# Banded depthwise 3D convolution: three of four channel blocks on TensorE instead of two of three, tile transfers split in four, turns spread over the unit

## The reference

```
def dsconv3d(x, dw_w, dw_b, pw_w, pw_b):
    y = jax.lax.conv_general_dilated(x, dw_w, (1, 1, 1), [(1, 1)] * 3, ..., feature_group_count=x.shape[1])
    y = jax.nn.gelu(y + dw_b[None, :, None, None, None], approximate=False)
    y = jnp.einsum('bcdhw,oc->bodhw', y, pw_w) + pw_b[None, :, None, None, None]
    return y
...
    xg = dsconv3d(xg, p['dw1_w'], p['dw1_b'], p['pw1_w'], p['pw1_b'])
    xg = dsconv3d(xg, p['dw2_w'], p['dw2_b'], p['pw2_w'], p['pw2_b'])
```

## Time and profile before

| | us |
|---|---|
| median of 3 runs | 19247.6 (19228.68 to 19251.41) |
| the profiled execution | 19248.37 |
| its span, first to last instruction | 19246.6 |
| first issue of dw1 to first issue of the next stage | 6046.46 to 6400.70 |
| the same for dw2 | 6598.58 to 7820.44 |

### The profile page before, as it was taken

How to read it: one execution, slowest core, us unless ns; L and a number is a source line. 1 busy time by engine, 2 the same in 40 slices (tenths; PEclk the granted TensorE clock), 3 DMA queues, 4 the chain that set the end, 5 groups by cost and what they waited for, 6 DMA issues and landing times. The chain is left out here.

```text
span 19246.6 us, 270014 instructions
## 1 busy us (share of the span) xinstructions
PE 16951.7 (88%) x77576; PEld 10108.8 (53%) x77576; DVE 16299.4 (85%) x12434; ACT 15364.9 (80%) x24406; POOL 12882.4 (67%) x6390
## 2 busy tenths in 40 slices
PE   8799997899985565798899999999999999989798
PEld 3455553555542244344466666666666666547374
DVE  4799998899975276378899999999999999979798
ACT  7699996899962444476699999999999999835556
POOL 0199991799952265154499999999999999800101
PEclk9899998999987787899999999999999999999899
DMA  5788876787886543656633333333333333352313
GB/s 176 233 241 242 247 242 211 236 243 236 251 228 187 194 139 135 223 214 257 266 112 111 111 112 117 112 111 118 116 111 112 117 112 111 111 160 57 103 52 98
DMA packets 857608, 3157.91 MB, mean 164 GB/s; under 512 B 106166, under 2 KB 139674, under 8 KB 831644
## 3 DMA queue, kind: packets, MB, share of 16 engines
q1 hardware_dynamic: 842396, 3091.03, 50.0%
q10 hardware_dynamic: 13824, 50.34, 0.7%
HBM read 2335.65 MB, written 805.32 MB: 163 GB/s over the span
## 5 line engine op out<-in xcount | busy, mean ns | idle before, releaser
L1929 DVE TENSOR_TENSOR_SCAN l1s_h<-l1s_da,l1s_pd 128x1024 f32<-128x1024 f32 x3072 | 6783.1, 2268 | 236.9 <-PE l1s_pd L1861 161.4
L1972 ACT ACTIVATE l1s_dm<-l1s_dut,l1s_bt 128x384 f32<-128x384 f32 x7424 | 4061.7, 605 | 74.8 <-PE l1s_pd L1861 74.6
L1955 ACT ACTIVATE l1s_da<-l1s_dl,l1s_a 128x1024 f32<-128x1024 f32 x3072 | 3502.0, 1140 | 30.7 <-DVE l1s_h L1929 29.6
L1861 PE MATMUL l1s_pd<-l1s_id,l1s_dm 128*128 128x128 f32 x22272 | 2973.0, 275 | 36.3 <-DVE l1s_h L1929 33.9
L1861 PEld LDWEIGHTS l1s_pd<-l1s_id,l1s_dm 128*128 128x128 f32 x22272 | 2562.1, 142 | 492.0 <-issue 288.2
L1835 POOL TENSOR_TENSOR l1s_pb<-l1s_h,l1s_cc 128x1024 f32<-128x1024 f32 x1024 | 2519.5, 2460 | 86.1 <-DVE l1s_h L1929 75.6
L1839 POOL TENSOR_TENSOR l1s_pa<-l1s_sm,l1s_cc 128x1024 f32<-128x1024 f32 x1024 | 2435.2, 2378 | 0.0
L1872 PE MATMUL l1s_py<-l1s_pb,l1s_both 128*128 128x512 f32 x4096 | 2157.2, 608 | 193.7 <-POOL l1s_pb L1835 193.5
L1830 POOL TENSOR_TENSOR l1s_sm<-l1s_h 128x1024 f32<-128x1024 f32 x928 | 2204.7, 2376 | 130.2 <-DVE l1s_h L1929 130.1
L1872 PE MATMUL l1s_py<-l1s_pa,l1s_id 128*128 128x512 f32 x4096 | 2114.4, 598 | 0.3 <-POOL l1s_pa L1839 0.3
L2795 POOL TENSOR_TENSOR l0sf_pr<-l0sf_h,l0sf_cc 128x1024 f32<-128x1024 f32 x768 | 1811.5, 2375 | 67.5 <-DVE l0sf_h L2877 52.7
(11 more groups left out here) (310 smaller groups left out, 31634.3 us busy)
## 6 DMA issues: line engine op xcount, KB each, us to landing
l1s_cc<-crows SPq DMA_DIRECT2D x1024, 512.0 KB, 3.7
l0sf_cc<-l0crowsf SPq DMA_DIRECT2D x512, 512.0 KB, 5.4
l0sb_cc<-l0crowsb SPq DMA_DIRECT2D x512, 512.0 KB, 5.4
l0sf_cc<-l0crowsf SPq DMA_DIRECT2D x512, 256.0 KB, 7.1
l0sb_cc<-l0crowsb SPq DMA_DIRECT2D x512, 256.0 KB, 7.0
dls<-l1p_dl SPq DMA_DIRECT2D x192, 512.0 KB, 6.9
duts<-l1p_dut SPq DMA_DIRECT2D x64, 1536.0 KB, 5.9
l1s_dut<-duts SPq DMA_DIRECT2D x64, 1536.0 KB, 7.2
```

The lines of the kernel that those rows point to most:

```text
L1861: mm = pe.transpose(pd[:, s % 2, blk * 128:blk * 128 + 128], dm[:, rnd % 2, blk, j * 128:j * 128 + 128], idt[:, :])
L1929: dve.tensor_tensor_scan(h[:, s % 4, :], da[:, j, :], pd[:, s % 2, :], 0.0, ALU.mult, ALU.add)\
L1955: act.activation(da[:, j, :], dl[:, half, j, :], ACT.Exp, scale=a[:, HT * half + j, n:n + 1])\
L1972: ins = act.activation(dm[:, rnd % 2, blk, :], dut[:, half, blk, :], ACT.Identity, scale=bt[:, half, blk, n:n + 1])
```

## The change

- dw2 takes blocks in steps of four, three through TensorE and one beside (`per_step` = 3, `steps` = 3); dw1 keeps two and one (`per_step` = 2, `steps` = 1). Of a middle frame's taps, ScalarE makes 12 products instead of 11 and VectorE does 14.
- Each tile or frame is loaded and stored by four DMAs of 32 rows instead of one.
- `xin` holds groups of 4 channels, with the 4 innermost: the turn in writes four floats in a row, and a matmul reads its moving operand at a step of 4 floats (16 bytes).
- `stg` is a ring of three half-units of 16 channels. In every third unit TensorE takes the channels from 16 on first (`in_order`), so that its halves lie in order in the ring.
- VectorE's turn-backs are spread, one about every 0.06 of a unit, and turns in are placed by the share of taps done.
- Buffers: weights 3 slots (loaded two pairs ahead), `prod` 3, `ot` 2, `vol` a ring of 6. The first tiles of a stage land in `raw`, `ot` and `sm`.
- SP's slices now run over the whole step (`SLICES`), with frames at shares of it.

```diff
-        share = 11 if len(depths) == 3 else 7
+        share = 12 if len(depths) == 3 else 7
...
+    def in_order(u, n):
+        return (n + 16) % 32 if u % 3 == 1 else n
...
-        xin = r.sb("xin", [128, 2, 32, T, SIDE])
-        stg = r.sb("stg", [128, 32, T, SIDE])
+        xin = r.sb("xin", [128, 2, 8, T, SIDE, 4])
+        stg = r.sb("stg", [128, 3, 16, T, SIDE])
...
-                        sp.dma_start(raw[:, q % RAWS, :], four_frames(src, q // T, q % T)).then_inc(s_raw[q % RAWS], 16)
+                        for rows, image, of in four_frames(q // T, q % T):
+                            sp.dma_start(to[rows, :], src[image, of, :]).then_inc(sem, 16)
...
-                        sp.dma_start(four_frames(dst, u, t), ot[:, q % OUTS, :]).then_inc(s_ot[q % OUTS], 16)
+                        for rows, image, of in four_frames(u, t):
+                            sp.dma_start(dst[image, of, :], ot[rows, q % OUTS, :]).then_inc(s_ot[q % OUTS], 16)
...
+                        load_weights(PAIRS * u + w + 2)
+                        if w % 2 == 0:
+                            load_raw(T * (u + 1) + w // 2 + 1)
+                        if 2 <= w < 10:
+                            store_tile(u - 1, w - 2)
...
-                                             x[:, c, :, ys.start + y:ys.stop + y], start=(y == 0), stop=(y == 1))
+                                             x[:, c // 4, :, ys.start + y:ys.stop + y, c % 4], start=(y == 0), stop=(y == 1))
...
-                    if c == 0 and u:
+                    if n == 0 and u > 1:
+                        act.wait_ge(back, nth(T * (u - 1) - 1))
+                    if n == 16 and u:
                         act.wait_ge(back, nth(T * u - 1))
...
+                        share = (n + 1) * per_step / TAPS + per_step * i
+                        while outs < T * UNITS and share >= outs // T + 1 + 0.06 + 0.06 * (outs % T):
+                            turn_back(outs)
+                            outs += 1
+                        while share >= ins // T - 1 + (ins % T + 1) / T and ins < T * UNITS:
+                            turn_in(ins)
+                            ins += 1
...
-    volume_conv(nc, "dw1", n2, g1, w["dw1_band"], w["dw1_edge"], w["dw1_bias"], w["dw1_taps"], 1, ACT.Gelu)
+    volume_conv(nc, "dw1", n2, g1, w["dw1_band"], w["dw1_edge"], w["dw1_bias"], w["dw1_taps"], 1, 2, ACT.Gelu)
...
-                w["dw2_band"], w["dw2_edge"], w["dw2_bias"], w["dw2_taps"], 4, ACT.Gelu)
+                w["dw2_band"], w["dw2_edge"], w["dw2_bias"], w["dw2_taps"], 3, 3, ACT.Gelu)
```

More of the change, by code:

```diff
@@ L933, in _, with volume_conv @@
                                 merge(f + 1)
-def volume_conv(nc, stage, src, dst, band, edge, bias, taps_w, steps, func):
+def volume_conv(nc, stage, src, dst, band, edge, bias, taps_w, steps, per_step, func):
     T = 8
-    PAIRS, SLOTS = 16, 4
-    PRODS, RAWS, OUTS = 4, 2, 3
-    UNITS = 2 * steps
+    PAIRS, SLOTS = 16, 3
+    PRODS, RAWS, OUTS, RING = 3, 2, 2, 6
+    UNITS = per_step * steps
     near = (0, -1, 1)
@@ L1058, in _ @@
+                load_raw(7)
+                for f in range(3, RING):
                     load_frame(0, f)
                 load_raw(8)
[L1060 to L1072, removed]
+                SLICES = PAIRS * per_step
@@ L1189, in _ @@
                             passed += 1
-                    while out < 32:
-                        evacuate(u, out)
+                    while out < CHANNELS * (i + 1):
+                        evacuate(out)
                         out += 1
@@ L1270, in _ @@
                             merge(i, f + 1)
-                        if (n - start) % 6 == 5 and turned_in < T:
-                            turn_in(u + 1, turned_in)
-                            turned_in += 1
-                for t in range(T):
-                    turn_back(UNITS - 1, t)
+                        share = (n + 1) * per_step / TAPS + per_step * i
[5 more added lines that the diff above has]
+                            ins += 1
+                while outs < T * UNITS:
+                    turn_back(outs)
+                    outs += 1
 def l0_expand(nc, g1, w, hid):
@@ L3090, in volume_tables @@
                 band[:, of, :, :, :, to] = rows[of - to + 1]
-        flat = blocks[:, 2].repeat(4, axis=0).reshape(steps, 4, 32, 27).reshape(steps, 128, 27)
-        parts = offsets.reshape(steps, 3, 32)
-        last = parts[:, 2].repeat(4, axis=0).reshape(steps, 128, 1)
-        return {"band": band.reshape(steps * 32, 128, 2, 3, 128), "edge": np.stack([rows[2], rows[0]], 1),
-                "bias": np.broadcast_to(parts[:, :2].reshape(1, steps * 2, 32), (128, steps * 2, 32)),
-                "taps": cat([flat, last], 2).swapaxes(0, 1)}
-    for name in ("dw1", "dw2"):
-        for part, table in volume_tables(v[f"L0_conv_{name}_w"], v[f"L0_conv_{name}_b"]).items():
+        parts = offsets.reshape(steps, per_step + 1, 32)
+        last = cat([blocks[:, per_step], parts[:, per_step, :, None]], 2)
+        bias = parts[:, :per_step].reshape(1, steps * per_step, 32)
+        return {"band": band.reshape(pairs, 128, 2, 3, 128), "edge": np.stack([rows[2], rows[0]], 1),
+                "bias": np.broadcast_to(bias, (128, steps * per_step, 32)),
+                "taps": last[:, None].repeat(4, axis=1).reshape(steps, 128, 28).swapaxes(0, 1)}
+    for name, per_step in (("dw1", 2), ("dw2", 3)):
+        for part, table in volume_tables(v[f"L0_conv_{name}_w"], v[f"L0_conv_{name}_b"], per_step).items():
             w[f"{name}_{part}"] = table
```

228 lines of the change are left out of this document (131 added, 97 removed).

## The result

The changed kernel takes 19292.6 us (median of 8 runs, 19269.82 to 19312.66), the kernel before beside it 19225.6 us: a ratio of 1.0032 with a 95% interval of 1.0021 to 1.0043. It is slower by 0.3%, where 18775 us and "faster" were forecast. The profiled execution has a span of 19310.4 us against 19246.6.

A forecast was written before the change was run, and what follows sets the result against it. It took dw1 and dw2 as bound by waiting, no engine full. dw2 at 30 + 3 x 245 + 57 = 822 us (-400) and dw1 at 282 (-72) took 19248.4 to about 18775 us, range 18640 to 18960.

The forecast's parts named there:

- The others per step: Busy time per dw2 step beside VectorE: GpSimd 193 us, ScalarE 150, TensorE 107 at full clock or 214 at 1.2 GHz.
- both fit below 223: TensorE's 107 us a dw2 step at full clock and 214 at 1.2 GHz both stay under VectorE's 223.
- VectorE sets the step: In dw2, VectorE's 223 us of work determines the step's length, with GpSimd 30 us below.
- the size of the 16-byte step: TensorE's strided reads cost none to a doubling; nearest row x1.6, 172 us a step at full clock, still covered.
- TensorE's growing instructions: Sign of being wrong: TensorE's own instructions grow, where channels were expected at 1.115 us in a full-clock stretch.
- C: Rival: the strided read doubles TensorE's time to 214 us a step at full clock; step about 270, total 18860; chance 0.12.
- D: Rival: doubled read meets the low clock, TensorE 428 us a step, total 19415; loss beyond a 402 us step; chance 0.03.
- Rival F: The four DMAs per tile do not spread: 320 us of tile transfers a step, total 19060; chance 0.06.
- VectorE per step: VectorE's busy time in a dw2 step from taps, merges and turns, with turns in at 1.96 us: 223 us.
- Rival E: VectorE's turn in falls to a plain pass: 19 us less per step, total 18715; chance 0.12.
- The waits: VectorE's waits in a dw2 step, from SP's backlog: 22 us within bounds 0 to 72, making the step 245 us.
- The edges: Start and end of dw2: 30 us to the first tap, 57 us after the last merge, guessed between 50 and 65.

The follow-up runs named there:

- h1: e1 with one DMA per tile and frame again instead of four: 19372.3 us, 1.0079 to the kernel before.
- i1: The kernel before with one edit, four DMAs of 32 rows per tile and frame for loads and stores: 18754.8 us, ratio 0.9757.
- e1: The changed kernel with xin in groups of 1 channel, so TensorE reads at a step of 4 bytes instead of 16: 18778.0 us, 0.9765 to the kernel before.
- e2: The changed kernel with xin in groups of 2 channels, a step of 8 bytes instead of 16: 18779.0 us, 0.9768 to the kernel before.
- h4: e2 with the three weight DMAs of a pair of channels as one of 576 KB: 18809.5 us, 0.9786 to the kernel before.
- h2: e1 with dw2 in steps of three blocks again, two of them on TensorE: 18855.9 us, 0.9810 to the kernel before.

## Why the prediction was wrong

**The first step that failed is TensorE's term under "The others per step".** It reads the group of 12 edge and 6 own records in the earlier trace rows as two channels and gets 107 us for 96. It is one channel: 214 us. The same page held what contradicts it. The earlier trace rows give TensorE 669.9 us and 4608 records in dw2; 8 units x 32 channels x 9 matmuls are 2304, half of that, and 669.9 / 256 is 2.6 us a channel (part of it at the low clock), not 1.1. Dividing the busy time by the known count of work would have shown it. So "both fit below 223" was false at the low clock (428 us) and barely true at the full one. With it failed "VectorE sets the step".

**The second is the size of the 16-byte step.** The bound was right (none to a doubling); the value within it, x1.6 from the strided turn, was too low: the channel measured x1.92. With the right base, even x1.6 would have given some 343 us a step and not 172, and could not have been called covered. The two errors multiply: 411 us against the forecast's 172. The prediction named TensorE's growing instructions as the sign of being wrong, and that is the sign that came.

**The rivals.** C named the mechanism, a doubled read, with half the price. D named the price: 428 us a step, and 411 were measured. Its break-even of 402 us a step, 4.2 us per channel, leaves dw1 at the forecast's 282 us, though D itself has dw1 grow to 373; with dw1 growing in step it is (1576 - 175) / 3.67 = 382 us, 4.0 per channel. The measured 4.29 is above both. But D's cause was the low clock, and the clock was granted in full, as the forecast argued. With the base right, C would have been D, and the strided read at full clock the likeliest case. D's 19415 is above the measured 19293: 3 x 17 us of the difference are dw2's steps at 428 against 411.

**The transfers were right, and undervalued.** 512 KB in four DMAs spread: at dw2's start, where only loads run, the changed kernel moves 233 GB/s, against 105 in the earlier trace rows.

```profile
6581.00:6595.00 14.00, 0.00 (x0) 0.00 (x0) 3.52 (x3) 3.31 (x3) 1.97 (x1) 0.50 1.04 233
```

Rival F, that they don't, is out. The forecast priced their absence at 19060 and h1 measured 19372. i1 shows that this part alone carries the whole gain, 459 us. The Trainium skill's advice against splitting a transfer over parts of the partitions ("DMA: Bandwidth & Descriptors", Rules for kernel authors) does not hold for this source, which has four images outermost, and which moved 105 GB/s at a DMA share of 0.26 as one DMA: here the measurement decides, 18755 to 19214 us. What holds is the Trainium skill's rule in the same section that the prediction went by, on an outermost dimension below 16.

**VectorE per step was right in its own terms.** 223 us were forecast for turns in of 1.96 us; e1 has 218 busy in its middle step and 1.97 us a turn. GpSimd was put at 193 and measured 196, ScalarE 150 and 144. Rival E was right that a turn in falls to nearly a plain pass (1.23 us against 1.18). In the new order it was worth nothing (e2 against e1), since VectorE alone was not the bound.

**The waits were too low, for another reason than the one given.** 22 us a step, from SP's backlog, were forecast, for a step of 245 us; e1's steps take 262 and 284. The second is TensorE's 235 busy and 42 for weights (the prediction had it covered "as long as it needs less than the 5 us per pair"; it needs 4.5 and waits). VectorE waited 47 us in that step for output buffers, above the 30 that the prediction named as a sign of being wrong. SP issues at 0.45 to 0.47 us, as forecast, and its issues were not the limit (h4).

**The edges** were forecast at 30 and 57 us and measured 31 and 35 (7842.27 to 7877.04) in the changed kernel: all eight turn-backs stand behind the last merge, as put, in four pairs:

```profile
7845.08 3.73 DVE L1275 STREAM_TRANSPOSE dw_ot<-dw_stg 128x1024 f32<-128x1024 f32 x2 [0.46 <-ACT dw_stg L1177]
7850.88 3.68 DVE L1275 STREAM_TRANSPOSE dw_ot<-dw_stg 128x1024 f32<-128x1024 f32 x2 [2.08 <-DMA g<-dw_ot]
```

A round is 5.8 us where 6.8 were put, and the next stage's first issue comes 11 us behind the last pair. The rest of the 57 us was guessed from the 63 of before, and is not there.

**That e1 gives 18778 against the forecast's 18775 is luck in part.** dw1 is 17 us shorter and dw2 45 longer than forecast, and the program's other stages make up the rest. What it does show is that without the 16-byte step the change would have gained 2.35%. The mechanism of the forecast, VectorE setting the step, is not what gave that time.

**Where the gain of the new order went.** At 4 bytes the new order and the old are equal (18778 and 18755 us, intervals that overlap). Three of four blocks on TensorE gain 87 us of dw2 (h2 to e1), and the rest of the new order loses 95 there and 18 in dw1 (i1 to h2). Part of that loss is the third slot of weights: with four slots as in i1, the new order's dw2 takes 838 us against 859 (832 against 839 at 8 bytes), and dw1's 18 us take that back. The 12th product adds 14 us to GpSimd in each step, up to the 193 us that the forecast had for it.

## What to carry to other kernels

Before a period in a timeline becomes a price, divide the stage's busy time by the number of channels (or tiles) in it: records and instructions of the source need not be one to one, and a factor of two hides well in a group that repeats. When a change bundles several edits, run each alone: here one of them (four DMAs per tile) held all of the gain, one (groups of 4 channels) a loss of 515 us, and the rest nearly cancelled out. When waits are spread over many engines, look first whether they all have one slow transfer at their end; a faster transfer shortened the burst of turn-backs more than spreading it did.

## What the runs showed that was not expected

- A step of 8 bytes in TensorE's moving operand costs 6% of a channel (2.36 us against 2.23) and one of 16 bytes 92% (4.29 us); 32 bytes cost hardly more than 16 (a median of 634 against 624 ns a record).
- VectorE's turn in falls from 1.97 to 1.23 us as soon as it writes runs of two floats (e2), and runs of four or eight add nothing (1.23 in both). The turn back, which reads its source at a stride and writes whole rows, stays at 1.91 to 1.98 us. Runs of two floats thus get all of VectorE's gain at almost none of TensorE's loss.
- The same edit of the step costs 148 us in the kernel before and 515 in the changed one; the same edit of the transfers gains 459 us in the order before and 594 in the new one. No part has a price of its own.
- One transfer of 576 KB in the place of 384 KB and two of 24 KB lands 1.9 us later (5.1 against 3.2, h4 and e2), and the stores beside it 1.0 us later, at a DMA share of 0.73 against 0.69.
